# One low-half subtraction per expert moved from Pool to VectorE in a two-layer attention and mixture-of-experts kernel

## What is computed

```python
# layer 0: each token goes to 2 of 8 experts, at most 560 tokens per expert
h = gelu(einsum('ecd,edf->ecf', xg, w1) + b1)      # 560 x 256 by 256 x 1024
y = einsum('ecf,efd->ecd', h, w2) + b2             # 560 x 1024 by 1024 x 256
out = segment_sum(y * g)                           # scattered back to the tokens
# layer 1: each token goes to 2 of 8 experts
h = silu(einsum('th,ehf->etf', x, w1)) * einsum('th,ehf->etf', x, w3)
out = einsum('etf,efh,te->th', h, w2, w)
```

## Time and profile before

| | |
|---|---|
| median of three executions | 1095.21 us (1092.34 to 1095.92) |
| the profiled execution: its own time | 1098.09 us |
| the profiled execution: span of its records | 1095.9 us |
| layer 0's experts (first hidden matmul to the last row block) | 410 to 633 us of the span |
| layer 1's experts | 776 to 1088 us of the span |
| PE busy over the span | 939.3 us, 86% |
| DVE, ACT, Pool busy | 682.5, 545.6, 480.0 us |

### The profile page before, as it was taken

One profiled execution on the slowest core, in us unless ns is written; L12 is line 12 of the kernel. 1 busy time (PEld: TensorE's weight loads), 2 busy tenths in 40 slices (PEclk: granted clock), 3 DMA queues, 4 the chain that ended last, 5 costly groups with the idle time before them and its releaser, 6 DMA issues. The chain is left out here.

```text
span 1095.9 us, 22844 instructions
## 1 busy us (share of the span) xinstructions
PE 939.3 (86%) x7879; PEld 853.7 (78%) x7879; DVE 682.5 (62%) x1931; ACT 545.6 (50%) x1208; POOL 480.0 (44%) x462
## 2 busy tenths in 40 slices
PE   5889998998899839999999936872799999999997
PEld 4778877877787629898889914662799999999977
DVE  5556565675566557666666625756567777778533
ACT  3778877887788725555555513430234333433221
POOL 2123134142413235666666731356354565456423
PEclk9999998999999859999999968985799999999999
DMA  7878787886576047667766686642543453345101
GB/s 187 172 204 207 184 201 190 222 202 146 148 171 156 28 129 216 166 173 171 172 173 165 137 205 158 179 151 89 191 116 84 114 145 101 101 114 135 18 7 22
DMA packets 110020, 160.22 MB, mean 146 GB/s; under 512 B 11584, under 2 KB 98976, under 8 KB 107968
## 3 DMA queue, kind: packets, MB, share of 16 engines
q1 hardware_dynamic: 95952, 140.16, 48.9%
q0 software_dynamic: 13936, 18.33, 8.3%
HBM read 103.45 MB, written 56.96 MB: 146 GB/s over the span
## 5 line engine op out<-in xcount | busy, mean ns | idle before, releaser
L312 PE MATMUL ps<-XGH,WH 128*128 128x280 f32 (+1 forms) x768 | 223.0, 290 | 16.3 <-ACT GT L836 12.3
L312 PE MATMUL ps<-XGL,WH 128*128 128x280 f32 (+1 forms) x768 | 222.2, 289 | 0.0
L312 PE MATMUL ps<-XGH,WL 128*128 128x280 f32 (+1 forms) x768 | 221.7, 289 | 0.0
L1595 POOL TENSOR_TENSOR HTL<-GT,HTH 128x280 fp32r<-128x280 f32 x128 | 132.9, 1062 | 165.9 <-DVE HTH L1335 165.9
L1207 DVE CUSTOM_DVE_ANT_0 NS<-ps,negm 112x375 f32<-112x375 f32 x256 | 138.0, 545 | 108.4 <-PE ps L418 96.6
L312 PEld LDWEIGHTS ps<-XGH,WH 128*128 128x128 f32 x768 | 148.3, 193 | 21.4 <-ACT GT L836 17.0
L764 ACT ACTIVATE PP<-NS,MN 112x375 f32<-112x375 f32 x256 | 156.4, 611 | 3.2 <-DVE MN L1207 2.7
L312 PE MATMUL ps<-WH,HTH 128*128 128x256 f32 (+1 forms) x536 | 152.4, 284 | 2.0 <-DVE YY L1350 2.0
L426 PE MATMUL ps<-cst,PP 112*125 112x112 f32 x768 | 138.9, 291 | 17.4 <-ACT PP L764 14.5
L312 PE MATMUL ps<-WL,HTH 128*128 128x256 f32 (+1 forms) x536 | 150.5, 281 | 0.0
L312 PE MATMUL ps<-WH,HTL 128*128 128x256 f32 (+1 forms) x536 | 149.9, 280 | 0.0
(11 more groups left out here) (211 smaller groups left out, 1881.7 us busy)
## 6 DMA issues: line engine op xcount, KB each, us to landing
WG<-in_v SPq DMA_DIRECT2D x48, 512.0 KB
KST<-k_scratch SPq DMA_DIRECT2D x48, 376.0 KB, 5.5
WG<-in_w SPq DMA_DIRECT2D x32, 512.0 KB
k_scratch<-KHL SPq DMA_DIRECT2D x64, 188.0 KB
CT<-in_ctx_t SPq DMA_DIRECT2D x32, 375.0 KB, 7.0
xg_scratch<-zero SPq DMA_DIRECT2D x8, 1289.8 KB, 10.3
xg_scratch<-zero SPq DMA_DIRECT2D x16, 586.2 KB, 9.0
XG<-xg_scratch SPq DMA_DIRECT2D x14, 536.0 KB, 3.7
```

The costliest lines, as they stand in the source:

```text
L312: m = e.matmul(out_ap, l, r, start=n == 0, stop=n == len(steps) - 1)
L1595: e.tensor_tensor(HTL[:, f, cols], GT[:, gi % 3, :], HTH[:, f, cols], ALU.subtract).then_inc(hl_pool[layer], 1)
```

## The change

The low half of block 1 of every expert (the second of its 16 activated blocks) is made by DVE, right behind the cast of that block. Pool makes the other seven odd blocks. The counts in `hl_of`, which ACT and PE wait on, follow. It holds for both layers, so for 16 blocks in all. Nothing else is moved.

```diff
+        def by_pool(gi):
+            return gi % 2 == 1 and gi % 16 != 1
+
         def hl_of(gi):
-            return gi // 2 + 1, (gi + 1) // 2
+            pool = sum(by_pool(i) for i in range(gi + 1))
+            return gi + 1 - pool, pool
...
                 e.tensor_copy(HTH[:, f, cols], g).then_inc(hh[layer], 1)
-                if gi % 2 == 0:
+                if not by_pool(gi):
                     e.wait_ge(hh[layer], gi + 1)
                     e.tensor_tensor(HTL[:, f, cols], g, HTH[:, f, cols], ALU.subtract).then_inc(hl_dve[layer], 1)
...
                     for f in range(8):
-                        if f % 2:
+                        if by_pool((ex * 2 + hf) * 8 + f):
                             halves_lo((ex * 2 + hf) * 8 + f)
```

More of the change, by code:

```diff
@@ L538, in rows_out @@
                 if c in (0, 2):
-                    by_dve, by_pool = hl_of((ex * 2 + c // 2) * 8 + 7)
-                    e.wait_ge(hl_dve[layer], by_dve)
-                    e.wait_ge(hl_pool[layer], by_pool)
+                    n_dve, n_pool = hl_of((ex * 2 + c // 2) * 8 + 7)
+                    e.wait_ge(hl_dve[layer], n_dve)
+                    e.wait_ge(hl_pool[layer], n_pool)
                 pairs = []
@@ L830, in activated @@
                 if gi >= 3:
[L831 to L834, removed]
+                    n_dve, n_pool = hl_of(gi - 3)
+                    e.wait_ge(hl_dve[layer], n_dve)
+                    if n_pool:
+                        e.wait_ge(hl_pool[layer], n_pool)
                 if layer == 0:
```

## The result

The changed kernel is faster: 1090.35 us median (1081.51 to 1095.21, 20 runs) against 1095.93 us (1091.26 to 1102.63, 20 runs) for the kernel before. The ratio of the means is 0.9941, 95% interval 0.9923 to 0.9959, which is 6.5 us, between 4.5 and 8.4 (the medians alone differ by 5.6). The forecast was 9.8 us. So "faster" and the range of 1080 to 1091.5 held; the size was too large by half and lies outside the interval, the median is outside the 1082 to 1089 of the likeliest case, and it is next to the 1090.4 of the first rival, in which Pool's next low half takes over the wait.

What follows compares the result with a forecast made beforehand. Layer 0's hidden phases were taken as bound by late Pool and a serial DVE-Pool line; six experts by 1.58 (9.5 us) plus 0.3 for expert 7 made 9.8 us off 1095.21: 1085.4 us, range 1080 to 1091.5.

Steps and rivals of the forecast that it cites:

- the first rival: Layer 0: ACT waits for block 3 instead of block 1; only 0.75 us per expert returns, 1090.4 us; chance 0.14.
- DVE's added low halves fit into idle time: Each costs 0.45 or 0.46 us, ahead of DVE's idle 2.82 us in layer 0 and 0.76 us in layer 1.
- The wait moves from block 4 to block 6: Layer 0, experts 1 to 6: ACT's 2.1 us wait at block 4 goes, with a shorter one at block 6.
- What DVE does in the gap: Layer 0: DVE's casts of blocks 4 and 5 and block 4's low half, 1.05 us, run while Pool ends its DMA.
- the serial line: Layer 0: back-to-back DVE and Pool work to the first drained row block ends 1.58 us earlier; six experts, 9.5 us.
- Pool is as late in the next expert as it was.: Layer 0: Pool's DMA chain follows the constant 12.31 us rows phase, so each expert's gain adds up.
- Expert 7: Layer 0's last expert: the moved half shortens the serial line there too; between 0 and 0.9, taken as 0.3 us.
- A low half on DVE costs Pool's DMA nothing: Pool's row DMAs beside DVE's low half keep 1.55 us; cost put at nothing.
- PE as the bound: Rival for layer 0's hidden phases: PE's stall goes nearly whole, about 15 us, giving 1080 us; chance 0.08.
- its three instructions: Layer 0's gap: DVE's casts of blocks 4 and 5 and low half of block 4, 0.30 + 0.45 + 0.30 us.
- The turn-taking total: Within the no-change rival (chance 0.07): only the serial line's total counts, saving 0.34 us per expert, 2 to 3 us.
- The landing of the next rows: Layer 0: next expert's rows land by 480.3, just when needed if transposes come 1.6 earlier; tight, no median bound.

Runs made afterwards that it cites:

- e1: Block 1's low half to DVE in layer 0 only, layer 1 as in the kernel before: ratio to before 0.9905, expert stretch 174.45 us.
- e2: Block 1's low half to DVE in layer 1 only, layer 0 as in the kernel before: ratio to before 0.9978, expert stretch 179.87 us.
- e8: The kernel before with its engine-picking rule rewritten, same instructions, every odd block on Pool: ratio to before 1.0025, expert stretch 179.93 us.
- e4: The changed kernel plus a wait: in layer 0 Pool's block 3 low half follows DVE's of block 4; ratio to before 0.9900, stretch 170.86 us.
- e11: The kernel before with Pool's weight chunk made by DVE behind the fourth row block's drain, experts 0 to 6 of layer 0: ratio 0.9972, stretch 177.77 us.
- e3: Block 9's low half to DVE in place of block 1's, otherwise as the kernel before: ratio to before 0.9951, expert stretch 178.52 us.
- e6: All low halves of layer 0 on DVE, layer 1's odd blocks on Pool as in the kernel before: ratio to before 0.9896, stretch 165.90 us.

## Why the prediction was right, and where it was not

- **Where the time is.** Right: hidden phases of layer 0, nothing in the rows phases and nothing in layer 1 (e1, e2, and 12.34 beside 12.31 us).
- **DVE's added low halves fit into idle time.** Right: e2 shows it for layer 1. In layer 0 the gap of 2.82 us before the cast of block 4 is down to 0.21.
- **The wait moves from block 4 to block 6.** Right: 1.74 us at block 6, as the rows after show. It does not take over in full, and the phases shorten by 0.5 to 1.1 us (expert 1 by 1.31 from before, which had the lower clock there, and by 0.82 from e8, which had not). The signs given for being right asked for more, phases of 12.8 to 13.3 us; none of the six is there.
- **"What DVE does in the gap" and "the serial line".** The term that was mis-sized: 1.58 us for each of six experts, 9.5 us. Where DVE's weight chunk stands behind Pool's last row DMA, it measured 1.10 in four experts and 0.76 in two, 5.9 us. With 0.6 for expert 7 that is 6.5, less 0.8 for the next point, and 0.5 for the clock in expert 1 of before: the 6.2 of the stretch. I had block 4's cast and low half and block 5's cast run while Pool ended its DMA; in the changed kernel one of them is always caught behind Pool's next low half. e4 takes that away and gets 2.4 us back. The row that tells of it was in the trace of before, in expert 7: a cast recorded at 1.63 us from 609.58, though Pool's row DMA ran until 610.21 and its low half could only follow. I did not read it.

```profile
609.58 1.63 DVE L1335 CAST HTH<-GT 128x280 fp32r<-128x280 f32 x1 [0.39 <-issue]
```

```profile
608.69 1.52 POOL L1607 DMA_INDIRECT x_scratch<-YY,XG  x1 [0.30 <-issue]
```

- **"Pool is as late in the next expert as it was."** Right to within 0.16 us in five experts, by the end of its last row DMA behind the phase's start. In expert 2 it is 0.60 later than before; the comparison there is with the short phase behind the one at the lower clock.
- **Expert 7.** 0.61 us for 0.3 forecast, a guess between 0 and 0.9.
- **A low half on DVE costs Pool's DMA nothing.** Right for the moved one, by luck of its place: no row DMA of experts 1 to 6 starts while it runs. As a rule it does not hold, see the last section: where a row DMA starts during block 0's low half it takes 1.70 to 1.71 us, in experts 2 and 3 of the changed kernel and already in expert 5 of before. The term was taken from a DMA that had started first.
- **Pool is late because of the weight chunk.** I had named the chunk and the row DMAs together. The chunk has some 1.1 of the 6.4 us in it, the row DMAs the rest (e11). It had no term in the sum.
- **Rivals.** PE as the bound (15 us) is out. The next low half taking over the wait (4.8 us) is nearly as close to the measured 6.2 of the stretch as the lower end of the forecast, 6.5, and inside the interval of the whole runs. Its condition, that DVE doesn't get its three instructions done in the gap, came true in all six experts. In experts 1 and 5 none of the three was done and the gain is 0.76, that rival's 0.75; in the other four only the cast of block 4 was, and it is 1.10, between its 0.75 and the forecast's 1.58. The truth lies between the two, and I had given them 0.14 and 0.66. The turn-taking total alone gives 0.9 us (e3), so it isn't the mechanism, and the term of 0.34 us per expert was still too high. The landing of the next rows, which I called tight, costs PE up to 1.7 us in a phase once Pool is out of the way (e6).

## What to carry to other kernels

When an engine is late only at one point of a loop, move the first thing it does there, and look at what its next instruction will then shut out: a low half moved from the middle of the phase gave 0.9 us where the first one gave 6.2. A wait added at that point can be worth more than it costs. And the longest instruction in a late engine's queue costs only what it takes beyond the wait that it fills: check when the ones behind it had their inputs. Here a chunk of 2.98 us made Pool 1.1 us late.

## What the runs showed that I had not expected

**A Pool instruction keeps DVE out before it runs.** With its predecessor, a row DMA, running for another 0.8 us, Pool's low half already kept a DVE low half out (1.95 us in place of 0.45; 0.45 in e4, beside the same DMA). In experts 1 and 5 it kept out a cast (1.49 and 1.74 us in place of 0.30).

**A DVE subtraction with both inputs in SBUF holds up an indirect DMA of Pool that starts during it.** In e11 the DMA at 443.96 begins 0.11 us after DVE's weight chunk (the timeline of DVE):

```profile
443.85 1.22 DVE L951 TENSOR_TENSOR WL<-WG,WH 128x1024 fp32r<-128x1024 f32 x1
```

It takes 2.53 us in place of 1.55, and so it does (2.46 to 2.53) in all five such places. In the changed kernel the DMA at 472.77 starts 0.17 us into a low half of DVE and takes 1.70. Where the DMA starts first, as in the earlier trace rows, it keeps its 1.55. A cast does it too, for the little that is left of it: the DMA at 525.19, with 0.20 us of a cast left, takes 1.62. The DMAs that start during an operation with one input in PSUM (the drains YY and the subtraction XGL) take 1.55 to 1.59. The Trainium skill (SBUF — State Buffer, "Who interferes with whom") gives as the reason why a tensor_tensor did not stall a DMA that it takes only the read interface while the writing of descriptors needs the write interface, and marks that as inferred; for these indirect DMAs it does hold them up. The same section has such a DVE instruction contend with Pool instructions that read SBUF, and this DMA's destination rows are given by numbers that lie in SBUF (XG), so that rule may be what is seen; no run here tells the two apart.
